# Feed-forward products and output projection issued as quarter steps, with a new order of the steps on every engine: one RWKV-style layer in fp32 on one core

## The reference

```python
xn = _ln(x, ln1_w, ln1_b); sx = _token_shift(xn, state[:, i1])
xxx = jnp.tanh((xn + sx * maa_x) @ maa_w1).reshape(b, l, 5, 1, EXTRA_MAA)
x5 = xn[:, :, None] + sx[:, :, None] * (maa_stack + jnp.matmul(xxx, maa_w2).reshape(b, l, 5, E))
w = jnp.exp(-jnp.exp(time_decay + jnp.tanh(x5[:, :, 1] @ decay_w1) @ decay_w2))
r, k, v = x5[:, :, 3] @ Wr.T, x5[:, :, 0] @ Wk.T, x5[:, :, 2] @ Wv.T
g = jax.nn.silu(x5[:, :, 4] @ Wg.T)
# per head, over tokens:  a = k_t v_t';  out = r_t (u * a + s);  s = a + w_t * s
att = group_norm(outs) * gn_w + gn_b
x = x + att * g @ Wo.T
xn2 = _ln(x, ln2_w, ln2_b); sx2 = _token_shift(xn2, state[:, i0])
xk, xr = xn2 + sx2 * ffn_maa_k, xn2 + sx2 * ffn_maa_r
rr = jax.nn.sigmoid(xr @ ffn_Wr.T); kk = jnp.square(jax.nn.relu(xk @ ffn_Wk.T))
x = x + rr * (kk @ ffn_Wv.T)
```

## Time and profile before

| | us |
|---|---|
| median of 3 runs | 795.95 (795.33 to 804.35) |
| the profiled execution, its own time | 795.61 |
| its span | 793.8 |
| busy PE, PEld | 705.9, 491.4 |
| busy DVE, ACT, POOL | 513.6, 324.7, 376.7 |

### The profile page before, as it was taken

How to read it: one execution, slowest core, us unless ns; L and a number is a source line. 1 busy time by engine, 2 the same in 40 slices (tenths; PEclk the granted TensorE clock), 3 DMA queues, 4 the chain that set the end, 5 groups by cost and what they waited for, 6 DMA issues and landing times.

```text
span 793.8 us, 17668 instructions
## 1 busy us (share of the span) xinstructions
PE 705.9 (89%) x7412; PEld 491.4 (62%) x7412; DVE 513.6 (65%) x767; ACT 324.7 (41%) x639; POOL 376.7 (47%) x223
## 2 busy tenths in 40 slices
PE   5986899997999889998799979998799978998797
PEld 4763677465674667556664665746665556755673
DVE  5638865695567774597556966677736965479441
ACT  2231843247332753427532483326433375325311
POOL 1248426763458435573257634584255732674000
PEclk9997899999999989999999999999999999999799
DMA  7910001010020201010010200202010000100000
GB/s 205 377 28 27 9 2 48 6 62 3 1 54 1 61 3 35 21 53 9 2 50 5 61 2 1 53 2 62 2 41 14 28 8 2 53 2 28 2 1 26
DMA packets 19275, 28.79 MB, mean 36 GB/s; under 512 B 5888, under 2 KB 11776, under 8 KB 18176
## 3 DMA queue, kind: packets, MB, share of 16 engines
q1 hardware_dynamic: 19200, 27.67, 11.0%
HBM read 18.35 MB, written 4.19 MB: 28 GB/s over the span
## 4 chain that ended last, share of the span: by engine, by line
PE 51%; issue 15%; POOL 14%; DVE 11%; ACT 7%; DMA 0%; POOLq 0%; DVEq 0%; ACTq 0%
PE FB L563 17%; PE BAB L820 7%; POOL pp L488 7%; PE FA L838 5%; PE FB L571 5%; PE FA L872 2%; ACT half L1048 2%; PE BAB L797 2%; PE FA L639 2%; DVE kvs L1357 2%; PE BAB L555 2%; PE FA L859 2%; PE BAB L733 2%; POOL mixes L453 2%; POOL mixes L451 1%
## 5 line engine op out<-in xcount | busy, mean ns | idle before, releaser
L488 POOL TENSOR_TENSOR pp<-rT,kT 128x2048 f32<-128x2048 f32 (+1 forms) x32 | 108.6, 3406 | 51.7 <-DVE rT L1229 51.7
L451 POOL TENSOR_TENSOR mixes<-mixes 128x1024 f32<-128x1024 f32 x30 | 72.0, 2400 | 127.9 <-ACT mixes L971 127.9
L453 POOL TENSOR_TENSOR mixes<-mixes,xnT 128x1024 f32<-128x1024 f32 x30 | 71.8, 2392 | 2.4
L563 PE MATMUL FB<-mixes,wk_s 128*128 128x256 f32 x256 | 66.1, 417 | 5.8 <-POOL mixes L453 3.5
L1321 DVE TENSOR_REDUCE half<-half 128x256 f32<-128x2048 f32 (+2 forms) x32 | 64.4, 2014 | 0.6
L504 POOL TENSOR_TENSOR acc<-acc,half 128x512 f32<-128x512 f32 x32 | 41.1, 1283 | 49.5 <-DVE half L1321 48.3
L563 PE MATMUL FB<-mixes,wv_s 128*128 128x256 f32 x256 | 60.8, 382 | 2.5 <-issue 1.5
L563 PE MATMUL FB<-mixes,wg_s 128*128 128x256 f32 x256 | 62.1, 392 | 0.0
L563 PEld LDWEIGHTS FB<-mixes,wk_s 128*128 128x128 f32 x256 | 52.1, 208 | 15.9 <-POOL mixes L453 4.5
L971 ACT ACTIVATE mixes<-FA,cols_s 128x256 f32<-128x256 f32 x116 | 45.4, 481 | 38.4 <-PE FA L639 33.4
L838 PE MATMUL FA<-wide,fk_s 128*128 128x256 f32 x256 | 57.2, 381 | 3.5 <-DVE wide L1472 2.2
(11 more groups left out here) (160 smaller groups left out, 1336.7 us busy)
## 6 DMA issues: line engine op xcount, KB each, us to landing
pp<-x SPq DMA_DIRECT2D x8, 512.0 KB, 3.8
xt<-x SPq DMA_DIRECT2D x8, 512.0 KB, 3.8
vp<-vT SPq DMA_DIRECT2D x128, 32.0 KB, 1.9
out<-wide SPq DMA_DIRECT2D x7, 512.0 KB, 3.0
wv_s<-wv SPq DMA_DIRECT2D x1, 1024.0 KB, 5.1
wk_s<-wk SPq DMA_DIRECT2D x1, 1024.0 KB, 7.6
wr_s<-wr SPq DMA_DIRECT2D x1, 1024.0 KB, 8.7
wg_s<-wg SPq DMA_DIRECT2D x1, 1024.0 KB, 10.8
```

The lines of the kernel that those rows point to most:

```text
L451: nc.gpsimd.tensor_tensor(slot, slot, sx, ALU.mult).then_inc(s_["mixm_ready"], 1)
L453: nc.gpsimd.tensor_tensor(slot, slot, xnT[:, :, 1:L + 1], ALU.add).then_inc(s_["mix_ready"], 1)
L488: ins = nc.gpsimd.tensor_tensor(pp[:, i % 2, 0:size].rearrange("p (n i j) -> p n i j", i=m, j=m), spread(r.unsqueeze(3), 3, m), spread(k.u ...
L563: ins = nc.tensor.matmul(dst[:, c * L:(c + 1) * L], weight[:, q, c * P:(c + 1) * P], src[:, q, :], start=(q == 0), stop=(q == C - 1))
```

## The change

On TensorE `c_fk` becomes four steps `c_fk0` to `c_fk3` of four matmuls, `c_fr` and `c_fv` four steps each of two matmuls (token half, then channel half), `b_wo` four steps of two (before: six and two). The matmuls, their operands and their waits stay the same in number and kind; in a token half of `c_fv` the second pair now waits for the second half of kk by itself. The lists of all engines are then written anew around the smaller steps. VectorE's list `main` stays as it was. The core of the diff, with the table cut to two places:

```diff
         main="""
-            c_fk b_score0 c_fr0 c_fr1 b_score1 c_fv0 b_score2 c_fv1 b_g0 b_score3 f_norm b_g1 b_score4 b_g2 b_g3
...
+            c_fk0 c_fk1 c_fk2 b_score0 c_fk3 c_fr00 c_fr01 c_fv00 b_score1 b_g0 c_fv01 c_fr10 b_score2 c_fr11
+            c_fv10 c_fv11 b_score3 f_norm b_g1 b_score4 b_g2 b_g3 b_vtok f_lora0 f_lora1 b_ktok f_m20 b_kv0
...
-                    for q, t in (((0, 0), (0, 1), (1, 0), (1, 1), (2, 0), (3, 0)), ((2, 1), (3, 1)))[part]:
+                    for q, t in (((0, 0), (0, 1)), ((1, 0), (1, 1)), ((2, 0), (3, 0)), ((2, 1), (3, 1)))[part]:
                         if t == 0:
                             pe.wait_ge(s_["y_ready"], C * b + q + 1)
...
-                    ins.then_inc(s_["wo_ready"], 1)
+                    if part >= 2:
+                        ins.then_inc(s_["wo_ready"], 1)
...
-            def c_fk(b, par, n):
-                loaded("fk")
-                for q in range(C):
+            def c_fk(q):
+                def run(b, par, n):
+                    if q == 0:
+                        loaded("fk")
                     pe.wait_ge(s_["xk_ready"], C * b + q + 1)
...
+            def token_half(dst, weight, src, t, h):
+
+                for q in (2 * h, 2 * h + 1):
+                    ins = nc.tensor.matmul(dst[:, t * E:(t + 1) * E], src[:, q, t * P:(t + 1) * P], big[weight][:, q, :],
+                                           start=(q == 0), stop=(q == C - 1), skip_group_check=True)
+                return ins
+
+            def c_fr(t, h):
+                def run(b, par, n):
+                    if h == 0:
+                        if t == 0:
+                            loaded("fr")
+                            pe.wait_ge(s_["xr_ready"], b + 1)
+                        if not last(b):
+                            pe.wait_ge(s_["r_ready"], 2 * b + 3 + t)
+                    ins = token_half(FB, "fr", xr, t, h)
+                    if h == 1:
+                        ins.then_inc(s_["fr_ready"], 1)
+                return run
...
+            def c_fv(t, h):
                 def run(b, par, n):
                     if t == 0:
-                        loaded("fr")
-                        pe.wait_ge(s_["xr_ready"], b + 1)
-                    if not last(b):
-                        pe.wait_ge(s_["r_ready"], 2 * b + 3 + t)
-                    project_tokens(FB, big["fr"], xr, [t]).then_inc(s_["fr_ready"], 1)
-                return run
...
+                        if h == 0:
+                            loaded("fv")
+                        pe.wait_ge(s_["kk_ready"], T * b + 1 + h)
+                    ins = token_half(FA, "fv", kk, t, h)
+                    if h == 1:
+                        ins.then_inc(s_["fv_ready"], 1)
                 return run
```

More of the change, by code:

```diff
@@ L52 @@
         first="""
-            f_norm warm6 f_lora1 f_lora0 f_pair1 f_m20 f_k0 f_k1 f_k2 f_k3 f_dec1 f_pair3 f_v0 f_v1 f_dec2 f_v2
+            f_norm warm6 f_lora1 f_lora0 f_pair1 f_m20 f_k0 f_k1 f_k2 f_v0 f_k3 f_dec1 f_pair3 f_v1 f_v2 f_dec2
             f_v3 f_r0 f_r1 f_r2 f_r3""".split(),
         second="""
-            b_score0 f_norm b_g0 b_score1 b_score2 b_score3 b_g1 b_score4 b_g2 b_g3 b_vtok f_lora0 f_lora1
-            b_ktok f_m20 b_kv0 b_kv1 f_m21 f_dec1 f_m22 f_dec2 b_acc b_apply0 b_apply1 f_k0 b_apply2 b_apply3
@@ L58 @@
-            f_k1 f_k2 f_v0 f_k3 f_m23 f_v1 b_gn0 b_gn1 f_v2 b_wo0 f_m24 b_wo1 f_r0 b_norm20 f_v3 f_r1 f_r2
-            b_norm21 f_r3""".split(),
+            b_g0 b_score0 f_norm b_g1 b_score1 b_g2 b_score2 b_score3 b_score4 b_g3 b_vtok f_lora0 f_lora1
+            b_ktok f_m20 b_kv0 b_kv1 f_m21 b_acc f_dec1 f_dec2 b_apply0 f_m22 b_apply1 b_apply2 b_apply3 f_k0
+            f_m23 f_k1 f_k2 f_v0 b_gn0 b_gn1 f_k3 f_v1 b_wo0 b_wo1 b_wo2 b_wo3 f_v2 f_m24 f_r0 f_v3 f_r1
+            b_norm20 b_norm21 f_r2 f_r3""".split(),
@@ L98 @@
         second="""
[L99 to L100 removed]
+            f_norm b_g0 b_rcopy b_g1 b_vtok f_lora0 f_lora1 b_ktok b_kv0 b_kv1 b_decays f_dec1 f_mix1 b_exp
+            f_mix2 f_dec2 b_sq0 b_sq1 f_k0 b_gn f_k1 f_v0 f_mix3 f_mix4 f_v1 f_r0 b_norm2 f_r1""".split(),
         main="""
[L102 removed]
@@ L103 @@
-            b_kv1 b_decays f_dec2 b_exp f_mix2 f_k0 b_sq0 b_sq1 f_k1 f_v0 b_gn f_mix3 f_mix4 f_v1 b_norm2 f_r0
+            c_fk0 c_fk1 c_fr0 c_fr1 f_norm b_g0 b_rcopy b_g1 b_vtok f_lora0 f_lora1 b_ktok b_decays b_kv0 f_mix1
+            f_dec1 b_kv1 f_dec2 b_exp f_mix2 b_sq0 b_sq1 f_k0 f_k1 b_gn f_v0 f_mix3 f_mix4 f_v1 f_r0 b_norm2
             f_r1""".split(),
         last="""
-            c_fk0 c_fk1 c_fr0 c_fr1 b_g0 b_g1 b_vtok b_ktok b_rcopy b_kv0 b_kv1 b_decays b_exp b_sq0 b_sq1 b_gn
+            c_fr0 c_fk0 c_fk1 b_g0 b_rcopy c_fr1 b_g1 b_vtok b_ktok b_kv0 b_kv1 b_decays b_exp b_sq0 b_sq1 b_gn
@@ L879, in _ @@
             for t in range(T):
-                steps.update({f"b_kv{t}": b_kv(t), f"b_gn{t}": b_gn(t), f"b_wo{t}": b_wo(t),
-                              f"b_norm2{t}": b_norm2(t), f"c_fv{t}": c_fv(t),
-                              f"c_fr{t}": c_fr(t)})
+                steps.update({f"b_kv{t}": b_kv(t), f"b_gn{t}": b_gn(t),
+                              f"b_norm2{t}": b_norm2(t)})
+                for h in range(2):
+                    steps.update({f"c_fv{t}{h}": c_fv(t, h), f"c_fr{t}{h}": c_fr(t, h)})
+            steps.update({f"b_wo{part}": b_wo(part) for part in range(4)})
+            steps.update({f"c_fk{q}": c_fk(q) for q in range(C)})
             steps.update(f_m20=f_m20, f_pair1=f_pair(1), f_pair3=f_pair(3))
```

39 lines of the change are left out of this document (15 added, 24 removed).

## The result

The changed kernel takes **805.35 us** (median of 6 runs, 801.80 to 813.16), the kernel before 799.69 us in the runs beside it (795.33 to 804.35). The ratio is **1.0105**, 95% interval 1.0063 to 1.0147: slower by 1%, within the 2% (the two medians alone lie 5.7 us apart, the ratio stands for 8.4 us). The forecast was 804 us, range 791 to 812. The profiled execution took 805.88 us with a span of 804.1 us, 10.3 us more than before; TensorE is busy for 709.3 us (before 705.9), VectorE for 529.2 us (before 513.6) though its work is the same.

The account below looks back on a forecast made before the run. TensorE was taken to bound the kernel, occupied 84.0 of 91.88 us per period, with a score chain setting the pace in places. 7.25 - 0.5 + 1.9 - 0.3 = 8.35 us on 795.61 us gave 804 us, range 791 to 812.

Parts of the forecast that it names:

- 7.25 us in the front half: `main`, score 0 to f_lora0: score 0 waits for prod0, f_lora0 comes 1.45 us later in each of five periods.
- about 1.1 in the rest: Terms outside the five periods: first period of `main` -0.5 us, `second` +1.9 us, `last` -0.3 us.
- An earlier start then changes nothing: GpSimd's prod0: makes no progress until VectorE's stream (xk, xr) is over, so copying r earlier leaves its end at 420.29.
- the forecast gap: TensorE before score 0: stands about 1.7 us waiting for prod0, in five periods; bounds 0.45 to 1.9 us.
- the replay: TensorE's new list stepped through from 420.4 with the old lengths: score 3 comes 1.7 us later, f_lora0 1.45 us.
- rival A: prod0: GpSimd gets in between VectorE's instructions, gap at score 0 is 0.45 us or none; 796.5 us; chance 0.26.
- its sign: Trace sign of rival A: prod0's first instruction at about 3 us, VectorE's L1472 group stretched.
- -0.5: First period of `main`: prod0 starts behind an early xk stream, no gap at score 0, f_xin free of f_sx; -0.5 us.
- +1.9: `second`: b_acc ahead of dec1 delays ScalarE's tanh, expansion and decay copy, so the first k group waits; +1.3 to +3, taken +1.9 us.
- Nothing behind it gives this back: `main` behind f_lora0: steps are released one by the other, so the delay stays; 1.8 us wait before the projection, no added cost.
- rival B: TensorE's clock: half of some ten new gaps bring a spell at 1.2 GHz, 1.69 us each; 812 us; chance 0.12.
- `last`: The part `last`: product after score 4 comes 1.7 us earlier, ScalarE's expansion of v starts as before; about -0.3 us.

Follow-up runs that it names:

- run 7: The control with the first half of TensorE's `main` in the new order and ScalarE's first copy of r ahead of the second norm: 797.23 us, ratio 1.0021.
- run 8: The control with the new second half of TensorE's `main`, GpSimd's new `main`, and ScalarE's new one except the move of r: 799.60 us, ratio 1.0037.
- run 3: The changed kernel with the list `main` put back to the old one on every engine: 802.37 us, ratio 1.0057.
- run 4: The changed kernel with ScalarE's second norm in `main` again ahead of the first half of r: 817.48 us, ratio 1.0217.
- run 6: The control with only the first half of TensorE's `main` in the new order, ScalarE as before: 804.12 us, ratio 1.0105.
- the control: New code with the smaller steps, every engine's old list with the pieces in their old places, against the kernel before: 798.02 us, ratio 0.9993.
- run 9: The kernel of run 3 with b_acc moved behind the two decay groups on TensorE in `second`: 797.34 us, ratio 1.0009.
- run 5: The control with ScalarE's copy of the first half of r moved ahead of the second norm in `main`: 795.97 us, ratio 0.9998.
- run 12: The control with TensorE's second group of k in `main` moved between the second and third group of applied states: 799.50 us, ratio 1.0033.

## Why the prediction was right and where it was wrong

- **Total and direction**: right, but the close total is luck. 8.35 us were forecast; 1.0105 is 8.4 us of 799.7. The terms differ: the forecast had 7.25 us in the front half, 0 in the back half and about 1.1 in the rest; measured are front half with r ahead 0.21%, back half 0.37%, `second` with `first` and `last` 0.57% (runs 7, 8, 3; each by itself uncertain by 0.2 to 0.3%), together 1.15% against 1.05% measured whole. A term too large by 5.5 us was made up by others too small by as much.
- **The failed step** is "An earlier start then changes nothing: prod0 still ends at 420.29". From two rows in which GpSimd waited I took who waits for a law. Runs 4 and 6 against the changed kernel and 7 show that the start decides it: GpSimd asking 0.35 to 0.53 us after the start of VectorE's six got in in all periods of these traces, asking 1.56 us or more after it never did. With the copy of r at its old place, the forecast gap, 1.0 to 1.7 us at f_lora0 (run 6 against the control) and the 93.2 us period all appear. So the arithmetic of the replay was right, and the term of 7.25 us was that of another kernel. It measured 1.7 us (run 7, 0.2 to 3.2 by the interval). This was rival A's mechanism, to which I gave 0.26; its sign (VectorE's group stretched) was the one named. A's own total of 796.5 us missed by 9 us, since it had the small terms for `second` and the back half too.
- **The first period and `second`**: -0.5 was wrong: the first period keeps a gap of 0.96 us ahead of score 0 (f_lora0 at 37.17 us, before 36.99), since ScalarE's late r in `second` puts the start of prod0 1.74 us behind the start of the six. +1.9 was too small: 4.5 us by run 3. The path was right (b_acc, tanh, mix, expansion, decay copy, first key group; forecast at 103.6 us, seen at 105.69), three sizes were off. VectorE's sum came 1.0 us late, behind the 1.75 us stop in the state products. b_acc and the first decay product were put at full clock and took 1.94 and 1.56 us, so the tanh started at 95.84 instead of 93.5. And the key group behind the wait ran at half clock, 3.54 us in place of 1.97. The stop may be chance in part: with the old list it measures 0 to 1.98 us from trace to trace, with the new one 1.54 to 2.30, and run 9 recovers with 2.30. No run varied it.
- **"Nothing behind it gives this back", back half 0**: right at full clock, with the 1.8 us gap ahead of the projection (1.78, 1.78, 1.61 us). In two periods of the loop run 8 is longer than the control by 1.65 and 2.93 us, with half clock behind the issue gaps, which I had not connected with f_m23. That is rival B's mechanism at a place that it didn't name.
- **Rival B's price** was too simple. A spell of 5.41 us on k0, k1 cost nothing in the loop's first half: the issue gaps behind it are smaller by as much (before, the first period took 92.78 us with the spell and gaps of 0.50 and 2.08, the third 93.07 with 3.72 and gaps of 1.70 and 2.36). A spell on k2, k3 behind the states can cost in full: the third period took 94.56 and 94.20 us with 5.41 there (runs 3, 5), 92.55 with 3.72 (control). But in the control's fourth and fifth period 5.18 and 5.16 cost at most 0.2 us (92.10 and 91.78).
- **`last`**: its period takes 0.11 us less, for a forecast of -0.3. The same old list gives 78.17 to 79.61 us from trace to trace, so this is not resolved.

## What to carry to other kernels

Before a wait is called fixed, ask what would happen if the waiting side came a microsecond earlier, and try that as one run; two rows with the same remainder show what happened, not what must. An order is a set of agreements between engines: one ScalarE copy was worth nothing that shows in the old order and 7 us in the new, and by the ratios either of two small edits gave back most of a part's loss, so sum no single-edit prices without the pair. When a term is replayed, time the part by itself (one half of a list) before the whole.

## What the hardware did that I had not expected

- In these traces VectorE and GpSimd exclude each other by whole instructions. Of VectorE's six instructions of 0.48 us one takes 2.57 us and the next 1.71 when GpSimd gets in; when not, GpSimd's first instruction is longer by its whole wait (2.92 us at 334.13, 3.71 at 692.55 in the earlier trace rows). The Trainium skill, "SBUF — State Buffer", section "SBUF: two separate sides", says that the two share a port pair as an exclusive lock held for the whole instruction, the first to start blocking the other; for VectorE it names among others the instructions with two SBUF inputs, as these are. The durations agree. What it doesn't tell is why GpSimd, asking at 692.55, passed the starts of three more VectorE instructions without its turn, while at 326.73 in the changed kernel it got it at the next. That next one, the first of xr, stands behind a semaphore wait in VectorE's program, the three others of xr don't; no run varied that, and it stays open.
- TensorE stands still inside 256 short matmuls where the profile shows nothing that it waits for: in the changed kernel 1.67 to 1.98 us at the same matmul in both turns of the loop (up to 2.36 elsewhere). Around the two gaps of the third period lies one 16 KB packet of the instruction queue each, begun 0.5 to 0.9 us before the gap. That TensorE ran out of instructions there is read from these traces; run 12 did not test it.
- "issue" in the idle column can be a data wait: 2.13 us in run 12, at the end of which VectorE's expansion had just finished.
